# First cross attention of a two-layer transformer block: value matmuls of four key chunks in a row, six exponential buffers

## What is computed

```python
qc = x @ w_q + b_q
kc = y @ w_k + b_k
vc = y @ w_v + b_v
scores = jnp.einsum('bhqd,bhkd->bhqk', qh, kh) / math.sqrt(D_HEAD)   # 16 heads of 8
attn = jax.nn.softmax(scores, axis=-1)
ca = jnp.einsum('bhqk,bhkd->bhqd', attn, vh) ... @ w_co + b_co
x = layer_norm(x + ca, ln_g, ln_b)
```

## Time and profile before

| | |
|---|---|
| median of 3 runs | 1106.84 us (1106.81 to 1107.83) |
| the profiled execution | 1106.37 us, span of the core 1104.6 us |
| granted TensorE clock, mean | 0.969 |
| first cross attention, bodies 0 to 15 | from 115.2 us to about 468 us of the span |
| TensorE, VectorE, ScalarE, GpSimd busy over the span | 1026.3, 748.1, 571.4, 389.8 us |

### The profile page before, as it was taken

How to read it: one execution, slowest core, us unless ns; L and a number is a source line. 1 busy time by engine, 2 the same in 40 slices (tenths; PEclk the granted TensorE clock), 3 DMA queues, 4 the chain that set the end, 5 groups by cost and what they waited for, 6 DMA issues and landing times. The chain is left out here.

```text
span 1104.6 us, 31648 instructions
## 1 busy us (share of the span) xinstructions
PE 1026.3 (93%) x12060; PEld 742.5 (67%) x12060; DVE 748.1 (68%) x1409; ACT 571.4 (52%) x1139; POOL 389.8 (35%) x273
## 2 busy tenths in 40 slices
PE   5977899999999999979688999999999999999997
PEld 2552577777777776646325777777777778777786
DVE  4657788887888778321794776777676767767752
ACT  2533577777777776631444544445444444544442
POOL 4821121111211123030105554545455454646542
PEclk9988899999999999989798999999999999999998
DMA  3501544444444443030002111111111111012100
GB/s 105 144 2 70 145 133 135 126 152 140 128 132 139 141 123 91 2 99 1 0 23 76 56 56 38 55 38 39 54 56 54 41 49 51 28 52 56 35 4 4
DMA packets 48461, 79.41 MB, mean 72 GB/s; under 512 B 8802, under 2 KB 35252, under 8 KB 48404
## 3 DMA queue, kind: packets, MB, share of 16 engines
q1 hardware_dynamic: 48404, 78.61, 23.8%
HBM read 51.13 MB, written 21.96 MB: 66 GB/s over the span
## 5 line engine op out<-in xcount | busy, mean ns | idle before, releaser
L1376 ACT ACTIVATE P<-PS 125x448 f32<-125x448 f32 x384 | 207.1, 544 | 270.3 <-PE PS L1285 268.4
L1266 POOL TENSOR_TENSOR Pl<-P 125x896 f16<-125x896 f32 x128 | 229.9, 1801 | 242.3 <-ACT P L1376 242.3
L1014 DVE TENSOR_REDUCE m<-PS 128x1 f32<-128x500 f32 x336 | 220.8, 675 | 120.1 <-PE PS L1005 118.3
L920 DVE TENSOR_REDUCE m_part<-PS 128x1 f32<-128x500 f32 x336 | 210.5, 673 | 54.8 <-PE PS L822 53.3
L1301 PE MATMUL PS<-cNh,P 125*128 125x97 f16 x1344 | 198.0, 208 | 0.1
L1303 PE MATMUL PS<-cNh,Pl 125*128 125x97 f16 x1344 | 197.4, 207 | 0.0
L1302 PE MATMUL PS<-cNl,P 125*128 125x96 f16 x1344 | 196.8, 206 | 0.0
L898 ACT ACTIVATE Pb<-PS 125x448 f32<-125x448 f32 x384 | 186.0, 547 | 19.5 <-PE PS L797 18.5
L1302 PEld LDWEIGHTS PS<-cNl,P 125*128 125x128 bf16 x1344 | 131.9, 98 | 25.5 <-issue 0.2
L1301 PEld LDWEIGHTS PS<-cNh,P 125*128 125x128 bf16 x1344 | 131.2, 98 | 15.8 <-issue 3.2
L1283 PE MATMUL PS<-Qh,cTh 110*125 110x448 f16 x384 | 139.0, 362 | 1.3 <-DVE Qh L1452 1.3
(11 more groups left out here) (170 smaller groups left out, 1530.0 us busy)
## 6 DMA issues: line engine op xcount, KB each, us to landing
Kst<-k_halves SPq DMA_DIRECT2D x144, 125.0 KB, 2.8
k_halves<-KH SPq DMA_DIRECT2D x16, 750.0 KB, 3.2
cx<-in_ctx SPq DMA_DIRECT2D x16, 562.5 KB
d_cx<-in_ctx SPq DMA_DIRECT2D x16, 562.5 KB
c_halves<-cHi SPq DMA_DIRECT2D x16, 281.2 KB, 2.6
c_halves<-cLo SPq DMA_DIRECT2D x16, 281.2 KB, 3.0
cTh<-c_halves SPq DMA_DIRECT2D x16, 281.2 KB, 3.0
cTl<-c_halves SPq DMA_DIRECT2D x16, 281.2 KB, 3.8
```

The lines of the kernel that those rows point to most:

```text
L920: nc.vector.tensor_reduce(m_part[:, t, part:part + 1], PS[:, 6 + k % 2, 0:SP], AX.X, ALU.max).then_inc(s_reduced, 1)
L1014: nc.vector.tensor_reduce(m21[:, t, part:part + 1], PS[:, S1[k % 2], 0:SP], AX.X, ALU.max).then_inc(n_red, 1)
L1266: nc.gpsimd.tensor_tensor(Pl[:, c % NP], P1[:, c % NP], high, ALU.subtract).then_inc(n_low_p, 1)
L1376: nc.scalar.activation(P1[:, c % NP, half * HALF:(half + 1) * HALF], PS[0:KC, u % 3, 0:HALF], ACT.Exp).then_inc(n_exp, 1)
```

## The change

`NPB` goes from 4 to 6. `values` of four chunks are issued behind each other at steps 5, 9 and 13 (chunks 0 to 3, 4 to 7, 8 to 11), in place of two at steps 3, 5, 7, 9, 11 and 13.

```diff
-        NPB = 4
+        NPB = 6
...
-                        if has_b and c % 2 == 1 and c >= LAG0 + 1:
-                            values(i, par, c - LAG0 - 1)
-                            values(i, par, c - LAG0)
+                        if has_b and c % 4 == 1 and c > LAG0:
+                            for ready in range(c - LAG0 - 3, c - LAG0 + 1):
+                                values(i, par, ready)
```

## The result

The changed kernel takes 1131.8 us (median of 4 runs, 1130.7 to 1133.3) against 1107.3 us before (median of 4 runs as well): 1.0221 times as long, 95% interval 1.0203 to 1.0238. The forecast was 1132.6 us, with a range of 1124 to 1141.

The account below looks back on a forecast made before the run. VectorE was taken to set the pace in steps 1 to 9, TensorE at step 9 and from L841 on. 23.5 (bodies 1 to 13), 2.4 (0 and 14) and 0.3 (15) sum to 26.2 us: 1106.37 to 1132.6, range 1124 to 1141.

Parts of the forecast that it names:

- bodies 1 to 13: Full bodies of the first cross attention: each 1.81 us longer, 23.5 us together.
- body 15: Last body, without pieces and set by ScalarE's exponentials: 0.3 us longer, taken between 0 and 1.5.
- Price of a block: Value matmuls on TensorE: four chunks take 1.74 us against 0.97 for two, 0.77 more; a merge saves 0.24 of edge.
- step 3: Block removed: of 1.01 us taken out of TensorE only 0.35 arrives at piece 10, VectorE eats the rest.
- step 5: Block doubled behind piece 10: +0.77, so piece 11 comes 0.42 us late; VectorE's gap grows from 0.29 to about 0.7.
- Step 7: Block removed: opens about 0.15 us of VectorE slack before piece 15, leaving +0.27 us from piece 15 to piece 18.
- Step 9: Block doubled with VectorE idle behind it: all 0.77 us counts, pieces 19 and 20 come 1.04 us late.
- Step 11: Block removed before L841: gain 0, L841 waits for the maxima 1.79 us behind piece 20, TensorE idle some 0.8 us.
- Step 13: Block doubled between L841 and the next body, covered by nothing: +0.77 us, next body 1.81 us late.
- Bodies 0 and 14: VectorE idles about 0.75 us before piece 15, so piece 15 comes 0.3 early: +1.2 us each, 2.4 together.
- Six buffers: Exponentials wait for the values of chunk c - 6, issued a step earlier: they cost nothing and are needed.
- rivals A to E: A TensorE-bound, 1095 us, 7%; B half, 1111, 5%; C nothing, 1107, 3%; D clock, 1172, 3%; E more stalls, 1140, 6%.

## Right and wrong, step by step

The starts of bodies 1, 14 and 15 before (body 0 is in the earlier trace rows, the last block in the earlier trace rows), and then of bodies 0, 1, 14 and 15 and the last block after:

```profile
139.17 0.60 PE L797 MATMUL PS<-Qst,Kst 110*125 110x224 f16 x4
...
433.41 0.60 PE L797 MATMUL PS<-Qst,Kst 110*125 110x224 f16 x4
...
453.56 0.79 PE L797 MATMUL PS<-Qst,Kst 110*125 110x224 f16 x6
```

```profile
117.61 0.98 PE L797 MATMUL PS<-Qst,Kst 110*125 110x224 f16 x4 [1.28 <-DMA Kst<-k_halves]
...
143.16 0.60 PE L797 MATMUL PS<-Qst,Kst 110*125 110x224 f16 x4
...
458.94 0.60 PE L797 MATMUL PS<-Qst,Kst 110*125 110x224 f16 x4
...
479.99 0.79 PE L797 MATMUL PS<-Qst,Kst 110*125 110x224 f16 x6
...
492.69 1.74 PE L808 MATMUL PS<-Pb,Vst 125*32 125x112 f32 x64
```

| | forecast | measured |
|---|---|---|
| body 0 | +1.2 | (143.16 - 117.61) - (139.17 - 115.24) = +1.62 |
| bodies 1 to 13 | 13 x 1.81 = +23.5 | 315.78 - 294.24 = +21.54, 1.66 each |
| body 14 | +1.2 | 21.05 - 20.15 = +0.90 |
| body 15 | +0.3 | 14.44 - 13.98 = +0.46 |
| sum | +26.2 | +24.5 |

The remaining 2.4 us between the two profiled executions (1133.32 against 1106.37) lie ahead of body 0, which starts at 117.61 instead of 115.24, in code that the change leaves alone and whose length scatters by more than that; the medians of the runs differ by 24.5 us.

*Price of a block, step 3, step 5.* Right to 0.04 us: x64 takes 1.74; with the 12.28 us between the bodies taken off, the key piece is at 257.63 (forecast 257.67), piece 10 at 260.63 (260.67), piece 11 at 263.26 (263.30). Of 1.01 us taken out of TensorE 0.39 arrive at piece 10.

*Step 7.* The term of a full body that was off. Piece 18 comes at 268.58, 0.14 us late in this body against the earlier trace rows, where 0.27 were forecast as the mean. The slack before piece 15 was put at 0.15: the forecast took the gap that the row showed, less 0.04 for a hand-over. It was about 0.3. The trace after has the reduction of piece 15 at 279.53, inside the 0.35 us that the two normalising operations from 279.26 take together: when the piece lies ready, VectorE starts it about 0.08 us before the end of the one in front. Those 0.08 us and the 0.04 taken off are most of the difference between 1.81 and 1.66 us a body. The merge at step 9 alone shows the same: expected was +0.57, measured +0.48.

*Step 9.* Right: VectorE's gap is 2.04 us, and from piece 18 to piece 19 it is 2.72 us where it was 1.96, +0.76.

*Step 11.* Right: L841 comes 286.01 - 284.18 = 1.83 us after piece 20, as before (1.84), with an idle TensorE of 0.74 us. The block removed there bought nothing, and its chunks are paid for again at step 13. This is the largest part of the change, 0.75 of 1.66 us a body; steps 3 to 9 make it slower by themselves.

*Step 13.* Right: with this merge alone +0.75, forecast 0.77.

*Bodies 0 and 14.* Taken as equal, and they are not. In body 14 piece 15 comes 0.62 us early rather than 0.3 (11.74 against 12.36 us from the body's start), since with no splits the earlier piece 10 helps too. In body 0 the third reduction starts 0.32 us later, counted from the body's start, than before (3.85 and 3.53 us); the granted clock over the first 4 us of the body is 0.53 where it was 0.62, so TensorE's return to full speed came later there. The three merges one by one, whose body 0 has the mean clock of the kernel before (0.94), lengthen it by 0.35, 0.05 and 0.76 us, 1.16 together against the 1.2 forecast. So the forecast of body 0 was right at an equal clock, and the rest of its +1.62 is mostly the clock.

*Six buffers, other engines, clock.* Nothing, as said. The granted clock is 1.00 in bodies 1 to 13 of both kernels, behind the wait of 0.74 us at L841 too, and rivals A to E did not happen.

*The total.* The time is within a microsecond of the forecast, and that is in part luck: the first cross attention grew by 24.5 us and not by 26.2, and the sum started from an execution 1.0 us below the median before (1106.37 against 1107.34).

## What to carry to other kernels

When two engines pace a loop in turn, price an edit of the order in each stretch by itself: merging work on the engine that is busy for 93% paid only where that engine set the pace both at the place that a block left and at the place that it came to (an edge, 0.24 us, and up to 0.30 measured), and cost 0.42 to 0.75 us a body elsewhere. Before a block is moved, look at what it covers: here it filled just the time that another engine needed for a serial chain, and L841 starts 1.84 us after piece 20 with the block and 1.83 without it. And when a long uninterrupted block is wanted, put it behind the last hand-over to the other engine; then six chunks in a row gained 0.7% here.

## What the runs showed of the hardware

The edge of a block was priced as one per block, but it depends on the neighbour. Behind score pieces (steps 3 to 9 of the kernel before) the trace shows 0.22 to 0.30 us of "issue" idle in front of the value matmuls' weight loads, and 0.17 behind the block. Next to the matmul that turns the maxima (14 output columns, to the PSUM partitions from 96 on), there is none on the side of the block, and the two interleave where the block comes second (L842 and L809 at 270.22 to 270.43). The Trainium skill (TensorEngine Tiling (Array Packing), Tiling Modes, Key Properties) says that changing the tiling mode drains TensorE. The rows agree with that if the 14-column and the 32-column matmuls count as the same mode, which no run here tests; no other width was tried either.

A VectorE operation that finds its input ready starts before its predecessor has ended in the trace: reductions of 0.67 us follow each other every 0.59 us (four in 2.42 us), across lines as well. Where the input comes just then, the overlap is lost, and with it some 0.08 us: in the kernel before, the four from piece 15 on start 0.14 us after L929 has ended, in the changed one 0.08 us before its end.
